# Forward row transform of a 2D DFT on one core: rows folded to half length, then turned with TensorE transposes

## The reference, cut to what matters

```
x = x + _L0_conv_ref(_gn(x), ...)
# layer 1, on v = _gn(x)
x_ft = jnp.fft.rfft2(v)
top = jnp.einsum('bixy,ioxy->boxy', x_ft[:, :, :m1, :m2], w1)
bot = jnp.einsum('bixy,ioxy->boxy', x_ft[:, :, -m1:, :m2], w2)
out_ft.at[:, :, :m1, :m2].set(top); out_ft.at[:, :, -m1:, :m2].set(bot)
x = x + jnp.fft.irfft2(out_ft, s=(h, w))
```

## Time and profile before

| what | value |
|---|---|
| three runs | 2806.41, 2804.49, 2798.95 us (median 2804.49) |
| profiled execution | 2809.89 us |
| its span, first to last instruction | 2808.1 us |
| mean granted TensorE clock | 0.963 |
| busy: PE, VectorE, ScalarE, GpSimd | 79%, 63%, 46%, 20% |

### The profile page before, as it was taken

The page is one execution under the profiler, slowest core; times in us unless marked ns, Lnnn a source line. Parts: engine busy times, 40 slices in busy tenths (PEclk is TensorE's granted clock), DMA queues, the critical chain, the costliest instruction groups (busy, mean ns, idle before and its releaser), DMA issues. The chain is left out here.

```text
span 2808.1 us, 37222 instructions
## 1 busy us (share of the span) xinstructions
PE 2221.9 (79%) x15026; PEld 1346.0 (48%) x15026; DVE 1756.9 (63%) x1704; ACT 1290.3 (46%) x1562; POOL 554.7 (20%) x427
## 2 busy tenths in 40 slices
...
GB/s 403 431 430 418 320 219 342 342 340 347 332 335 347 335 347 343 340 247 325 234 256 258 263 254 264 265 135 388 395 395 320 372 417 417 418 417 417 418 417 387
DMA packets 419767, 958.23 MB, mean 341 GB/s; under 512 B 13888, under 2 KB 325744, under 8 KB 375312
## 3 DMA queue, kind: packets, MB, share of 16 engines
...
## 5 line engine op out<-in xcount | busy, mean ns | idle before, releaser
L471 PE MATMUL psum<-mix_u,wcur 128*64 128x512 f32 x2048 | 881.9, 592 | 5.4 <-DVE mix_u L565 4.9
L471 PE MATMUL psum<-mix_v,wcur 128*64 128x512 f32 x2048 | 881.9, 592 | 0.0
L471 PEld LDWEIGHTS psum<-mix_u,wcur 128*64 128x64 f32 x2048 | 277.3, 136 | 596.1 <-issue 571.7
L1185 PE MATMUL psum<-tab_irow_icol,inv_t 128*128 128x512 f32 x1024 | 490.2, 602 | 50.0 <-ACT inv_t L1241 45.4
L1286 DVE TENSOR_TENSOR weights_or_rows<-weights_or_rows,psum 128x1024 f32<-128x1024 f32 x224 | 273.2, 1221 | 194.1 <-PE psum L1185 182.2
L1024 DVE COPY fwd_cols<-psum 128x544 f32<-128x544 f32 x128 | 141.8, 1108 | 396.8 <-PE psum L818 396.8
L818 PE MATMUL psum<-tab_frow_fcol_both_ident,fwd_x 128*128 128x128 f32 x3072 | 352.4, 276 | 4.2 <-DMA fwd_x<-x_scratch 4.2
L818 PEld LDWEIGHTS psum<-tab_frow_fcol_both_ident,fwd_x 128*128 128x128 f32 x3072 | 348.5, 193 | 5.5 <-DMA fwd_x<-x_scratch 4.3
L383 POOL COPY mix_v<-mix_u 64x2321 f32<-64x2321 f32 x128 | 339.4, 2652 | 26.6 <-PE psum L471 18.7
L729 DVE SCALAR_TENSOR_TENSOR tiles<-tiles 128x2048 f32<-128x2048 f32 x128 | 322.2, 2518 | 4.0
L510 ACT ACTIVATE tiles<-tiles,pcur 128x2048 f32<-128x2048 f32 x128 | 268.1, 2095 | 111.7 <-DVE tiles L729 105.1
(11 more groups left out here) (187 smaller groups left out, 1631.9 us busy)
## 6 DMA issues: line engine op xcount, KB each, us to landing
...
x_scratch<-tiles ACTq DMA_DIRECT2D x128, 1024.0 KB, 9.2
...
```

The lines of the kernel that those rows point to most:

```text
L471: last = nc.tensor.matmul(bank(k * 4 + q, 512, C, e * C), wcur[j][:, e, m * C:(m + 1) * C], taps[e][:, r0:r0 + 2, m:m + W], start=(m == 0) ...
L1185: last = nc.tensor.matmul(bank(n % 2 * 2 + a), TS[n % 2][:, a * P:(a + 1) * P], icol, start=True, stop=True)
```

## The change

Rows h and h + 128 of the image enter the transform with the same cosine and sine up to a sign: plus for even frequencies, minus for odd ones. So each half tile of four channels is first folded: VectorE adds the two row halves into `fwd_sum`, GpSimd subtracts them into `fwd_diff` (both 128 x 1024). The row matmul now has `frow` (64 wide, even or odd frequencies) as its stationary operand and 512 columns (2 channels x 256) of sum or diff as the moving one; even frequencies go to partitions 0 to 63 of one bank, odd ones to partitions 64 to 127. A group n is now two channels: two matmuls, 32 groups an image, 256 in all, PSUM banks 0 to 3. Since the result has frequencies on the partitions, a row copy (128 x 512, PSUM to `fwd_rows`) and four 128 x 128 transposes follow, into bank 4 or 5, and VectorE writes the turned data into `fwd_cols` with two copies of 128 x 136 a group. ScalarE makes the row copies of groups 0, 1, 2 of every four, VectorE that of group 3. Columns keep their calls but alternate between banks 6 and 7 (four banks before), so part m waits for the mode copy of part m-2. `junk` of the squares has one buffer instead of two, so every square waits for the one before.

The work is ordered in 128 steps u of two groups (four channels), 16 an image, two to a tile. PE in step u: rows of groups 2u+2 and 2u+3, transposes of 2u and 2u+1, and in odd steps u%16 = 1, 3, 5, 7, 9 a part of the columns of the image before. ScalarE: row copy 2u, a square, in even steps row copy 2u+1, a square; the store of modes at u%16 = 13. VectorE: row copy 2u+1 in odd steps, four turned copies of step u-1, the sum for step u+2.

```diff
-    frow = np.zeros((P, 2, P))
-    for half in range(2):
-        a = th * np.outer(np.arange(P) + half * P, np.arange(NM))
-        frow[:, half, :NM] = np.cos(a)
-        frow[:, half, NM2:NM2 + NM] = np.sin(a)
+    frow = np.zeros((P, 2, C))
+    for par in range(2):
+        k = np.arange(par, NM, 2)
+        a = th * np.outer(np.arange(P), k)
+        frow[:, par, :len(k)] = np.cos(a)
+        frow[:, par, NP:NP + len(k)] = np.sin(a)
     put("frow", frow.reshape(P, -1))
...
-            NX = 4
+            NX, NE = 4, 4
...
+            ED = [[sb(ph, f"fwd_{n}{i}", [P, CG // 2, W]) for n in ("sum", "diff")] for i in range(NE)]
+            RS = [sb(ph, f"fwd_rows{i}", [P, 512]) for i in range(4)]
...
-            junk = [sb(ph, f"fwd_junk{i}", [P, 2, 2 * W]) for i in range(2)]
+            junk = [sb(ph, f"fwd_junk{i}", [P, 2, 2 * W]) for i in range(1)]
...
+            def copied(n):
+                return (n + 1) // 4 if n % 4 == 3 else n + 1 - (n + 1) // 4
...
-                            sp.wait_ge(row_done, 2 * (t - NX + 1))
+                            sp.wait_ge(sums_done, 2 * (t - NX + 1))
+                            sp.wait_ge(diff_done, 2 * (t - NX + 1))
                             sp.wait_ge(sq_done, 4 * (t - NX + 1))
...
+                    def rows(n):
+                        if n % 2 == 0:
+                            pe.wait_ge(sums_done, n // 2 + 1)
+                            pe.wait_ge(diff_done, n // 2 + 1)
+                        if n >= 4:
+                            pe.wait_ge(row_dve if n % 4 == 3 else row_act, copied(n - 4))
+                        for par in range(2):
+                            last = nc.tensor.matmul(bank(n % 4, 512, C, par * C), frow[:, par, :],
+                                                    ED[n // 2 % NE][par][:, n % 2 * 2:n % 2 * 2 + 2, :],
+                                                    start=True, stop=True)
                         last.then_inc(row_done, 1)
+                    def transposes(n):
+                        pe.wait_ge(row_dve if n % 4 == 3 else row_act, copied(n))
+                        if n == 0:
+                            pe.wait_ge(n2, 4)
+                        if n >= 2:
+                            pe.wait_ge(tr_out, n - 1)
+                        for q in range(4):
+                            at = (4 + n % 2) * 512 + q * P
+                            last = nc.tensor.transpose(psum[:, at:at + P], RS[n % 4][:, q * P:(q + 1) * P], ident)
+                        last.then_inc(tr_done, 1)
...
-                            pe.wait_ge(row_out, c * NR + NR)
...
+                            pe.wait_ge(tr_out, (c + 1) * NR)
+                        if m == 1:
+                            pe.wait_ge(var_done, c + 1)
+                        if m == 2:
+                            pe.wait_ge(col_act, c * len(ON_ACT) + 1)
                         if m == 3:
-                            pe.wait_ge(var_done, c + 1)
+                            pe.wait_ge(col_dve, c * len(ON_DVE) + 1)
                         if m == 4:
-                            pe.wait_ge(col_act, c * len(ON_ACT) + 1)
+                            pe.wait_ge(col_act, c * len(ON_ACT) + 2)
                         for p in range(4 * m, min(4 * m + 4, 17)):
                             pair = 2 if p < 16 else 1
-                            at = (4 + m % 4) * 512 + p % 4 * P
+                            at = (6 + m % 2) * 512 + p % 4 * P
...
+                    rows(0)
+                    rows(1)
+                    for u in range(NU_):
+                        c, g, second = u // 16 - 1, u % 16 // 2, u % 2 == 1
+                        if u + 1 < NU_:
+                            rows(2 * u + 2)
+                            rows(2 * u + 3)
+                        transposes(2 * u)
+                        transposes(2 * u + 1)
+                        if c >= 0 and g == 0 and not second:
+                            norm(c)
+                        if c >= 0 and second and g < PARTS:
+                            columns(c, g)
...
+                    def square(t, g):
...
+                        if k >= 1:
+                            act.wait_ge(sq_done, k)
+                        nc.scalar.activation(junk[0][:, :, :],
+                                             XW[t % NX][:, :, 2 * g:2 * g + 2, :].rearrange("p a c w -> p a (c w)"),
+                                             ACT.Square,
+                                             accum_out=part[c % 2][:, k % GP:k % GP + 1]).then_inc(sq_done, 1)
...
+                    def row_copy(n):
+                        act.wait_ge(row_done, n + 1)
+                        if n >= 4:
+                            act.wait_ge(tr_done, n - 3)
+                        nc.scalar.activation(RS[n % 4][:, :], bank(n % 4), ACT.Copy).then_inc(row_act, 1)
...
+                    for g in range(4):
+                        square(0, g)
+                    for u in range(NU_):
+                        c, t, second = u // 16 - 1, u // 2, u % 2 == 1
+                        row_copy(2 * u)
+                        if t + 1 < B * NG:
+                            square(t + 1, u % 2 * 2)
+                        if u % 2 == 0:
+                            row_copy(2 * u + 1)
+                        if t + 1 < B * NG:
+                            square(t + 1, u % 2 * 2 + 1)
...
+                    def sums_of(h):
+                        t = h // 2
+                        dve.wait_ge(loaded[t % NX], loaded_by(t))
+                        if h >= NE:
+                            dve.wait_ge(row_done, 2 * (h - NE) + 2)
+                        half = slice(h % 2 * CG // 2, (h % 2 + 1) * CG // 2)
+                        v.tensor_tensor(ED[h % NE][0][:, :, :], XW[t % NX][:, 0, half, :], XW[t % NX][:, 1, half, :],
+                                        ALU.add).then_inc(sums_done, 1)
+                    def row_copy(n):
+                        dve.wait_ge(row_done, n + 1)
+                        if n >= 4:
+                            dve.wait_ge(tr_done, n - 3)
+                        v.tensor_copy(RS[n % 4][:, :], bank(n % 4)).then_inc(row_dve, 1)
+                    def turned(n):
+                        c, c0 = n // NR, n % NR * 2
...
+                        dve.wait_ge(tr_done, n + 1)
+                        src = bank(4 + n % 2).rearrange("p (c a m) -> p c a m", c=2, a=2)
+                        dst = A[c % 2][:, :, :, c0:c0 + 2].rearrange("p a m c -> p c a m")
+                        for par in range(2):
+                            last = v.tensor_copy(dst[:, :, :, par::2], src[:, :, :, par * C:par * C + 2 * NP])
+                        last.then_inc(tr_out, 1)
...
+                    for u in range(NU_ + 1):
+                        c, at = u // 16 - 1, u % 16
+                        if u < NU_:
+                            if u % 2 == 1:
+                                row_copy(2 * u + 1)
+                            if c >= 0 and at == 0:
+                                spread(c)
+                        if u >= 1:
+                            turned(2 * u - 2)
+                            turned(2 * u - 1)
+                        if u + 2 < NU_:
+                            sums_of(u + 2)
...
+                def _(pool):
+                    for h in range(2 * B * NG):
+                        t = h // 2
+                        pool.wait_ge(loaded[t % NX], loaded_by(t))
+                        if h >= NE:
+                            pool.wait_ge(row_done, 2 * (h - NE) + 2)
+                        half = slice(h % 2 * CG // 2, (h % 2 + 1) * CG // 2)
+                        nc.gpsimd.tensor_tensor(ED[h % NE][1][:, :, :], XW[t % NX][:, 0, half, :],
+                                                XW[t % NX][:, 1, half, :], ALU.subtract).then_inc(diff_done, 1)
```

102 lines of the change are left out of this document (30 added, 72 removed).

## The result

The change is 0.9% faster, little but clear of the spread between runs: 2778.64 us median (2772.05 to 2788.73, six runs) against 2802.86 (2798.95 to 2806.41, six runs), ratio 0.9913 with a 95% interval of 0.9894 to 0.9932. That is 24 us less, where 44 were forecast; 2778.64 lies inside the range, 18 us above the number.

What follows compares the result with a forecast made beforehand. PE, busy 70.00 of 70.00 us, bounded the kernel. Start 3.5, first image 52, seven images 471 (67.3 each) and last columns 16.5 make a block of 543 instead of 587 us: 2761, range 2735 to 2790.

Steps and rivals of the forecast that it cites:

- PE's terms: PE per step of four channels: rows 1.72, eight transposes 0.90, weight-width changes 0.21, together 2.83 us.
- long pair: Two steps (one tile) with a full column part: set by PE, 9.24 us plus 0.2 for waits.
- last columns: Column parts of the last image at the block's end: 16.5 us, as before.
- about 460 of 543: PE's busy time expected in the block, in us, down from all of 587.
- ScalarE's pair: ScalarE per pair of steps: four squares 4.16, three row copies 1.8, waits 0.1, sum 6.1 us.
- The short pair of 6.5: Two steps without columns: set by ScalarE (6.1), sum plus difference (6.4) or DMA (5.7), taken as 6.5 us.
- The start: Beginning of the block, until the chain fold, rows, copy is filled: 3.5 us.
- The store's charge of 3.3 an image: Once an image, the store's issues hold ScalarE 3.84 us, delaying row copies PE waits for; 3.3 charged.
- Mode copies ... lie in the shadow of columns: VectorE's mode copies, 1.74 us more in three pairs, were taken as covered by column calls.
- The blocking rival: VectorE's sums wait for GpSimd's differences; at a wait of 1 us, block 621 and total 2838 us; chance 0.12.
- The clock: Rival: PE not full in short pairs, clock falls to 1.2 GHz, adding 81 us: 2842; chance 0.04.
- Short and long pairs don't average: ScalarE can't work ahead in long pairs, as PE issues row matmuls only one step ahead; short pairs keep 6.5 us.

Runs made afterwards that it cites:

- the plain-matmul run: The changed kernel with its 1024 transposes as ordinary float32 matmuls with the identity: 2840.58 us, block 622.1.
- even columns: The changed kernel with column groups of four calls spread over most steps of an image, mode copies and store moved accordingly: 2772.57 us, ratio 0.9888.

## Why the prediction was right in sign and off in size

- **PE's terms held.** Rows 0.86 a pair of calls, transposes 0.93 to 1.02 for eight (0.90), long pair 9.36 (9.4), last columns 15.7 (16.5). The weakest one, 0.112 a transpose from a record count and a load slope, holds: eight take 0.93, and the plain-matmul run pays 0.118 more for each. PE is busy 511 of the block's 559 us. The "about 460 of 543" of the prediction does not come out of its own terms: 8 x 5.66 + 7 x (4 x 9.24 + 6.7 + 3 x 5.66) + 15.6 = 485. The run without the difference has 495; the rest of the 511 goes with records stretched by half clock.
- **ScalarE's pair was 5.74, not 6.1.** A copy takes 0.593 and a square 1.054, as taken, but the next instruction starts before the record of the one before has ended, so that a copy and a square with its accumulator reading come every 1.52 (the run without the difference, first image). Halving the squares changed nothing.
- **The short pair of 6.5 was right where nothing but sum and difference meets**: in the first image steps come every 3.32 us, 6.64 a pair. It is sum plus difference, 1.2 + 2.36 less a small overlap; the forecast had 1.2 + 2.0. In the other images the steps between column parts took PE's 2.89, not 3.32.
- **The start failed**: "3.5 until the chain fold, rows, copy is filled" took 10.0. The first rows do start after 3.5, but each sum then takes 3.3 against a difference, and PE, with nothing to do before, runs its first 6 us at half clock. That is 6.5 of the 16 us.
- **The store's charge of 3.3 an image failed**: moving it gave nothing. PE waits for VectorE there, not for ScalarE.
- **What stands in its place** is the term costed at nothing: VectorE's small operations. "Mode copies ... lie in the shadow of columns" holds for those out of PSUM. But the spreading copy (0.2 before, 2.12 in the mean after) and the one-element addition (0.15 before, 1.78 in the mean) each wait for a difference, behind them stand turned copies and sums, and both fall into steps that have no column calls as cover. Moving the spreading copy and rewriting the one-element operations gives 1.64 us an image, with the limits shown. In the image read above the loss stands in the steps around these two, and 2.5 of it is the half clock behind PE's idle time; how the rest divides between them, the longer sums next to them and the chain back to PE is not shown. It goes with the difference: 4.5 us above PE's need are left with both operations on VectorE, none without the difference.
- **The number was partly luck.** Without the false charge of 3.3 the forecast for an image is 64.0, 5.9 below a full one; the false charge and the short last interval hide most of that. The measured gain is little over half of the forecast one.
- **The blocking rival came true in part.** It had the gain gone at a wait of 1.25 us for each sum at the forecast's price of a turned copy, 0.7 at the dearer one. The sums waited 0.8 us in the mean (1.99 against 1.2), and the turned copies were cheaper than either: four start to start with what follows in 0.95, 0.24 each.
- **The clock** gave way to 0.81 at the end of an image, after PE's idle time, and cost 2.5 us in the image read above; over the whole block it is 0.96, against 1.00 before. The rival had it fall in all 29 short pairs. In those of the first image it is 1.00 (1280 to 1330 us, PE busy 44.94 of 50), and in the run without the difference, with every transpose in place, it is 1.00 with PE full. By the Trainium skill ("TensorE: Matmul & The Clock Gate", Part 4), transposes don't count as activity; no run here shows the clock fall because of them. Where it fell above, PE had idled 1.92 us ahead of a group of transposes and 1.55 behind it, so that the two can't be told apart there.
- **"Short and long pairs don't average" failed as stated**: in the change itself the steps between column parts are PE's 2.89, and with even columns every step with columns is PE's. Evening out gave only 1.2 us an image because the steps around the end of an image, where the loss is, stayed.
- **Of the 24 us in the medians**, the block explains 28.2 in the profiles. The 4 between them are less than unedited parts move from run to run: the edited block began between 1267.7 and 1274.5 us in the profiles of the changed kernel and its variants, and at 1279.2 in the profile before. What moves them was not looked into.
